# A gated message pass over 25,000 sorted edges: destination rows taken from the node pass by 0/1 products

## The reference

```python
h = jnp.maximum(_layernorm(x, axis=-1), 0.0)
concat = jnp.concatenate([h[src], h[dst], edge_attr], axis=-1)      # 96 + 96 + 64
gates = jax.nn.sigmoid(concat @ W_e + b_e)
messages = jax.nn.softplus(concat @ W_n + b_n)
gated = gates * messages
h_new = jax.ops.segment_sum(gated, dst, num_segments=n)
edge_count = jnp.clip(segment_sum(ones, dst), 1.0, None)
return x + h + h_new / edge_count
```

## Time and profile before

| what | value |
|---|---|
| three runs | 864.51, 865.22, 868.5 us; median 865.22 |
| the profiled execution | 866.81 us, of which the span is 865.0 us |
| busy share of the span | POOL 77%, ACT 67%, PE 66%, DVE 65% |
| mean granted TensorE clock | 0.741 of full speed |
| mean share of the 16 DMA engines | 36.8% on SP's queue q1, 10.7% on POOL's queue q0 |

### The profile page before, as it was taken

How to read it: one execution, slowest core, us unless ns; L and a number is a source line. 1 busy time by engine, 2 the same in 40 slices (tenths; PEclk the granted TensorE clock), 3 DMA queues, 4 the chain that set the end, 5 groups by cost and what they waited for, 6 DMA issues and landing times.

```text
span 865.0 us, 10598 instructions
## 1 busy us (share of the span) xinstructions
PE 569.3 (66%) x2360; PEld 447.4 (52%) x2360; DVE 560.8 (65%) x2397; ACT 583.2 (67%) x1475; POOL 668.3 (77%) x598
## 2 busy tenths in 40 slices
PE   0497775784666466988764665489966664569861
PEld 0376554564554355666553554367655543456650
DVE  5799977567756775677567756775577557754550
ACT  3699988757775777577757775777577756775440
POOL 4787778777777777777777877787778777877774
PEclk9999987768788777555788788755577788775575
DMA  6766655544554455445544554455445543532200
GB/s 215 218 208 192 190 183 147 189 126 125 152 187 125 125 155 184 125 124 149 189 128 123 152 186 127 125 147 189 129 124 147 187 129 125 159 99 80 72 31 23
DMA packets 67032, 125.23 MB, mean 145 GB/s; under 512 B 38167, under 2 KB 39049, under 8 KB 66968
## 3 DMA queue, kind: packets, MB, share of 16 engines
q1 hardware_dynamic: 47390, 96.48, 36.8%
q0 software_dynamic: 18816, 27.77, 10.7%
q10 hardware_dynamic: 762, 0.30, 0.1%
HBM read 77.50 MB, written 48.17 MB: 145 GB/s over the span
## 4 chain that ended last, share of the span: by engine, by line
POOL 74%; issue 20%; DMA 2%; POOLq 1%; DVE 1%; PE 0%; ACTq 0%; SPq 0%
POOL edge_x L324 53%; POOL out L341 22%; DMA out<-node_out 1%; DMA index_rows<-in_src 1%; POOLq L341 1%; DMA edge_x<-in_x,gather_idx 0%; POOLq L339 0%; DVE node_out L637 0%; DVE stats L663 0%; DVE final L575 0%; POOLq L321 0%; DVE softplus L705 0%; PE trans_ps L760 0%; ACTq L245 0%; DVE gather_idx L500 0%
## 5 line engine op out<-in xcount | busy, mean ns | idle before, releaser
L324 POOL DMA_INDIRECT edge_x<-in_x,gather_idx x392 | 469.1, 1197 | 128.2 <-issue 119.2
L398 ACT ACTIVATE node_out<-node_x,shift,rstd 128x96 f32<-128x96 f32 x686 | 279.0, 458 | 1.7 <-DVE shift L615 1.7
L793 PE MATMUL trans_ps<-ident,concat 128*128 128x128 f32 x392 | 92.7, 414 | 259.6 <-ACT concat L433 259.6
L341 POOL DMA_INDIRECT out<-final,scatter_idx x196 | 197.9, 1010 | 59.7 <-issue 58.5
L663 DVE BATCH_NORM_STATS2 stats<-edge_x 128x6 f32<-128x96 f32 x392 | 67.4, 245 | 258.6 <-DMA edge_x<-in_x,gather_idx 258.6
L809 PE MATMUL z_ps<-weights,concat_t 128*128 128x192 f32 x784 | 220.8, 414 | 0.0
L793 PEld LDWEIGHTS trans_ps<-ident,concat 128*128 128x128 f32 x392 | 73.9, 216 | 276.1 <-ACT concat L433 257.0
L809 PEld LDWEIGHTS z_ps<-weights,concat_t 128*128 128x128 f32 x784 | 151.1, 227 | 56.0 <-issue 56.0
L405 ACT ACTIVATE log_var<-var 128x24 f32<-128x24 f32 x51 | 11.4, 223 | 239.0 <-DVE var L685 239.0
L433 ACT ACTIVATE concat<-edge_x,shift,rstd 128x96 f32<-128x96 f32 x392 | 145.7, 456 | 2.7 <-DVE shift L615 0.7
L557 DVE BATCH_NORM_STATS2 stats<-node_x 128x6 f32<-128x96 f32 x784 | 142.6, 242 | 0.0
(11 more groups left out here) (68 smaller groups left out, 373.4 us busy)
## 6 DMA issues: line engine op xcount, KB each, us to landing
node_x<-in_x SPq DMA_DIRECT2D x49, 768.0 KB, 5.8
out<-node_out SPq DMA_DIRECT2D x49, 768.0 KB, 7.5
dst_across<-in_dst SPq DMA_DIRECT2D x48, 256.0 KB, 7.1
edge_x<-in_x,gather_idx POOLq DMA_INDIRECT x392
concat<-in_edge_attr SPq DMA_DIRECT2D x48, 128.0 KB, 6.3
out<-final,scatter_idx POOLq DMA_INDIRECT x196, 2.2
dst_across<-in_dst SPq DMA_DIRECT2D x1, 212.0 KB, 3.6
index_rows<-in_dst SPq DMA_DIRECT2D x2, 64.0 KB
```

Source lines behind the costliest of these rows:

```text
L324: nc.gpsimd.indirect_dma_start(out=edge_x[u][:, t, side, :], out_offset=None, in_=x, in_offset=bass.IndirectOffsetOnAxis(ap=gather_idx[:, ...
L341: nc.gpsimd.indirect_dma_start(out=out, in_=final[j % FINALS][:, t, :], in_offset=None, out_offset=bass.IndirectOffsetOnAxis(ap=scatter_id ...
L398: last = nc.scalar.activation(node_out[u][:, r, :], node_x[u][:, r, :], ACT.Relu, bias=shift[us][:, c:c + 1], scale=rstd[us][:, c:c + 1])
L793: last = nc.tensor.transpose(trans_ps[h][:, t, b, :], concat[uk][:, 2 * h + t, b * P:(b + 1) * P], ident[:, :])
```

## The change

- The gathers by `dst` go, with `base`. POOL issues four gathers a step, and `edge_x` holds only source rows.
- The scatters add to what the node pass has stored (`compute_op=ALU.add`) instead of overwriting, so the rows to write are the mean alone (one instruction, L717).
- h at the destinations comes from the node pass. A chunk is now laid out as 16 blocks of 128 consecutive nodes (block = row of the tile, node = partition). The low seven bits of each destination are stored once to `low_pad` and, for each half chunk, 400 of them from the first edge of the half on are copied to all partitions (`low_across`). DVE compares them with the partition's number (`one_hot`, 800 columns). PE multiplies each block of h (as stationary operand) with 64 columns of that 0/1 matrix (`picks`, L950), at an offset read from a table of places into registers, and ACT copies each half's 336 columns to `dst_t` (L502), in which h of the destination stands transposed for `z`.
- `z` is made of three products: source rows with a row of ones for the bias (97 rows, L1016), destination rows (96, L1017), attributes (128 rows, two tiles' worth with half of the weights zero, L1018).
- Node chunks are moved in pieces of one node row, 384 bytes, 2,048 for each chunk.
- `same_prev` compares only the last 32 edges of a tile with the first 32 of the next. `dst_across` has two buffers where it had four, and SP issues it for batch `i-7` where it was `i-3`. `LEAD` is 3, the node sum is a step further ahead, three node rows of 16 are DVE's.
- A start-up part finds where each block's edges begin (`places`), and the slow path computes its messages anew.

```diff
-LEAD = 2
+LEAD = 3
-BY_DVE = 2
+BY_DVE = 3
+WINDOW = 64
+REACH = 336
+SPAN = REACH + WINDOW
-            first = min(i * CHUNK, NODES - CHUNK)
-            return t[first:first + CHUNK, :].rearrange("(p r) d -> p r d", p=P)
+                parts = [(t[lo:lo + CHUNK, :].rearrange("(r p) d -> p r d", p=P), tile[:, :, :])]
...
+            def load_low(n):
+                first, second = (first_at(sp, first_row[0:1, 2 * n + h:2 * n + h + 1]) for h in range(2))
+                wait(sp, onehot_done, n)
+                for h, at in ((0, first), (1, second)):
+                    sp.dma_start(low_across[:, h, :],
+                                 low_flat[bass.ds(at, SPAN)].partition_broadcast(P)).then_inc(low_loaded, 16)
...
+                n = i - 2
+                if i >= NS - 1 and runs_step(n):
+                    load_low(n)
-                k, ok, uk = back(i, o, u, LEAD + 1)
+                k = i - 7
                 if runs_step(k):
-                    wait(sp, same_done, k - NS + 1)
+                    wait(sp, same_done, 2 * (k - 1))
...
-                    wait(pool, base_done, i - NS + 1)
+                    wait(pool, edge_norm_done, i - NS + 1)
                     for t in range(TB):
-                        for side in range(2):
-                            nc.gpsimd.indirect_dma_start(
-                                out=edge_x[u][:, t, side, :], out_offset=None, in_=x,
+                        nc.gpsimd.indirect_dma_start(
+                            out=edge_x[i % NS][:, t, :], out_offset=None, in_=x,
...
-                            bounds_check=NODES - 1, oob_is_err=False).then_inc(scattered[j % FINALS], 16)
+                            bounds_check=NODES - 1, oob_is_err=False, compute_op=ALU.add).then_inc(scattered[j % FINALS], 16)
...
+            def pick_columns(d, h, at):
+                wait(act, pick_done, 2 * d + h + 1)
+                nc.scalar.activation(dst_t[0:D, bass.ds(at, REACH)], pick_ps[0:D, 0:REACH], ACT.Copy).then_inc(pick_out, 1)
...
+            def one_hot(n):
+                wait(dve, low_loaded, 32 * (n + 1))
+                wait(dve, pick_done, 2 * (n - 1))
+                nc.vector.tensor_scalar(onehot[n % 2][:, :, :], low_across[:, :, :], lane[:, 0:1], None,
+                                        ALU.is_equal).then_inc(onehot_done, 1)
...
+                k, j, m = i - 1, i - 2, i - 3
+                c, n, d = i + LEAD, i - 1 + LEAD, i - 2 + LEAD
...
                 if now:
-                    last = node_stats(uc, 3, R)
-                if runs_step(k):
-                    nc.vector.tensor_tensor(base[uk][:, :, :], edge_x[uk][:, :, 1, :], concat[uk][:, :, D:2 * D],
-                                            ALU.add).then_inc(base_done, 1)
+                    last = node_stats(c, 3, R)
+                if runs_step(n):
+                    one_hot(n)
+                if runs_step(d):
+                    wait(dve, pick_done, 2 * d + 2)
+                    nc.vector.tensor_tensor(node_out[d % NS][:, :, :], node_out[d % NS][:, :, :], node_x[d % NS][:, :, :],
+                                            ALU.add).then_inc(node_sum_done, 1)
...
+            def picks(d, h, at):
+                wait(pe, pick_out, 2 * d + h)
+                for b in range(BLOCKS):
+                    a = at[h * BLOCKS + b]
+                    last = nc.tensor.matmul(pick_ps[0:D, bass.ds(a, WINDOW)], node_out[d % NS][:, h * BLOCKS + b, :],
+                                            onehot[d % 2][:, h, bass.ds(a, WINDOW)], start=True, stop=True)
+                last.then_inc(pick_done, 1)
...
-                            nc.tensor.matmul(z, ones[0:1, :], bias[0:1, :], start=True, stop=False)
-                            for b in range(2):
-                                last = nc.tensor.matmul(z, concat_t[:, h, t, b, :], weights[:, b, :], start=False, stop=(b == 1))
+                        nc.tensor.matmul(z, src_t[0:D + 1, t, :], w_src[0:D + 1, :], start=True, stop=False)
+                        nc.tensor.matmul(z, dst_t[0:D, e:e + P], w_dst[0:D, :], start=False, stop=False)
+                        last = nc.tensor.matmul(z, attr_t[:, t // 2, :], w_attr[t % 2][:, :], start=False, stop=True)
```

More of the change, by code:

```diff
@@ L218, in last_rows @@
             return i == STEPS - 1
-        def first_steps(step):
-            for i in range(-LEAD, 0):
-                step(i, i // NS, i % NS)
         def ends(i, passed):
@@ L298, in _ @@
+            for i in range(STEPS + 7):
+                step(i)
             for u in range(NS):
-                sp.wait_ge(node_stored[u], 16 * ((STEPS - 1 - u) // NS + 1))
+                sp.wait_ge(node_stored[u], chunk_dmas(STEPS - 1 - (STEPS - 1 - u) % NS))
         @block.gpsimd
@@ L762, in _ @@
                 nc.tensor.transpose(cols_ps[n][:, P:TILES], index_rows_f[0:k, n, 1, :], ident[0:k, 0:k]).then_inc(cols_done, 1)
-            pe.wait_ge(cols_read, 2)
-            pe.wait_ge(message_ones_done, 1)
-            pe.wait_ge(weights_loaded, 16 * 4)
+            pe.wait_ge(cols_read, 1)
+            nc.tensor.matmul(heads_ps, ones[0:1, :], dst_col[0:1, 1:1 + TILES], start=True, stop=True).then_inc(heads_done, 1)
+            place_regs = [pe.alloc_register(f"place{b}") for b in range(R)]
@@ new lines, in step @@
+                if runs_step(d):
+                    if d == 0:
+                        pe.wait_ge(place_loaded, 32)
+                        pe.wait_ge(ones_done, 2)
+                    pe.load(place_regs, place_row[0:1, d * R:(d + 1) * R])
+                    at = [pe.snap(r, min_val=0, max_val=REACH) for r in place_regs]
+                    wait(pe, node_norm_done, d + 1)
+                    wait(pe, dve_norm_done, d + 1)
+                    wait(pe, onehot_done, d + 1)
+                    picks(d, 0, at)
@@ L798, in step @@
+                    last.then_inc(attr_trans_done, 1)
+                if runs_step(d):
+                    picks(d, 1, at)
                 if runs_step(m) and not ends(i, 1):
@@ L812, in step, with later_sums @@
                     sums(i - 2)
-            steps(step, 2)
+            for i in range(-LEAD, STEPS + 2):
+                step(i)
             pe.wait_ge(flag_done, 1)
             bad = pe.value_load(flag[0:1, 0:1], min_val=0, max_val=1)
-            def tile_sums(t, n):
+            def later_sums(n):
                 pe.wait_ge(r_diag_done, n + 1)
```

790 lines of the change are left out of this document (500 added, 290 removed).

## The result

| | kernel before | changed kernel |
|---|---|---|
| median of runs | 865.8 us (864.51 to 868.5, 4 runs) | 949.6 us (948.0 to 955.4, 4 runs) |
| ratio | 1 | 1.098 (95% interval 1.092 to 1.103) |
| span of the profiled execution | 865.0 us | 949.3 us |
| granted clock, mean | 0.741 | 0.792 |

Ratios in this document leave out executions that took over 1.5% more than the fastest of the same kernel on the same chip, so they can differ a little from a ratio of medians.

The account below looks back on a forecast made before the run. SP's loop through DVE was to bound each step: 8.8 + 1.6 + 1.05 = 11.4 (L) plus 6.0 (M) = 17.4 us. Start 81, 42 rounds 731, three short 39, end 37: 888 us, 2.6% slower; range 800 to 1,000.

Parts of the forecast that it names:

- Loop through SP, T = L + M: SP and DVE: node sum to `dst_across` landing (L, 11.4 us) plus comparison to node sum (M, 6.0) makes 17.4 a step.
- L of before, 8.8 us: In the kernel before, `node_x` issue to `dst_across` landing, taken from the old trace as 8.8 us.
- Small pieces, +1.6 us at 22 ns a piece: Chunk loads and stores in 384-byte pieces: 256 on each DMA engine take 5.6 us against 4.05, adding 1.6 to L.
- The first rival: Small chunk pieces cost only their bytes, 15.8 ns each: L 9.9, T 15.8, total 811 us; chance 0.22.
- the price doubled for stores: Rival: chunk stores in 384-byte pieces cost twice 22 ns, adding 2.8 us a step, about 1,010 us in total; chance 0.07.
- `low_across`, +1.05 us: Two `low_across` loads in SP's queue, 0.41 MB at 388 GB/s, add 1.05 us to L.
- M = 6.0: DVE's work from the comparison to the node sum's end, 0/1 matrix included, takes 6.0 us (5.4 to 6.1).
- Register loads at nothing: SP's register loads fall while its queue is full of the store's pieces: no cost; without that cover up to 2 us.
- Adding scatters cost POOL no change: On POOL, a scatter that adds takes no longer than a plain one, about 1.0 us; upper bound 2.1.
- The start, 81: Start-up: first node sum at 42 us, three more by the loop through `low_across` at 13 us each, ending at 81.
- PE at the low clock: Rival: half of the steps take PE's low-clock 21.2 us, half 17.4, so T is 19.3 and the total 976; chance 0.17.
- Loop doesn't hold: Rival: `dst_across` lands in time, the loop through `low_across` sets 13.4 us a step, total 708 us; chance 0.10.

Follow-up runs that it names:

- three ways of opening it: Changed kernel with `dst_across` one step earlier, 797 us; with it ahead of `low_across`, 843; with both ahead of SP's wait for the node sum, 734 to 740.
- the first four experiments: Changed kernel: `dst_across` a step earlier, 796.7 us; `dst_across` ahead of `low_across`, 843.1; both ahead of SP's wait, 740.3; chunks in 6,144-byte pieces, 884.6.

## Why the prediction was half right

- **Loop through SP, T = L + M.** Right. The waits, the chain, SP's issue at the very end of each node sum, and three ways of opening it (797, 843 and 734 to 740 us) show it. POOL, ACT, DVE don't bind, as worked out; POOL's 12.3 us a step (12.8 by the scatters' measured 1.58) would have mattered only without the loop.
- **L of before, 8.8 us.** Right: 8.80 with both additions taken out, though it was put together from one step's issues and a median landing.
- **Small pieces, +1.6 us at 22 ns a piece.** Near, with some luck: 1.53 with `low_across` in the queue, 1.1 without. A chunk's pieces take 6.6 us of the engines and not 5.6 (22 ns is their median, 25.7 their mean), and in large pieces 5.3 and not 4.05, so both were too low and the difference is 1.3. This and `low_across` are why the share of q1 is 52.8% and not the 40 to 45 named as a sign. The first rival (pieces at the price of their bytes) is out. So is the price doubled for stores: it would have added 2.8 us, and the whole cost of loads and stores in small pieces is 1.5; the first half of a round's small pieces, the load in the queue's order, takes 25.2 ns each and the second, the store, 26.2. The Trainium skill's rule on transfers below 512 bytes (DMA: Bandwidth & Descriptors, section Specifications) is not contradicted in its direction, since large pieces are faster, but no doubling shows.
- **`low_across`, +1.05 us.** This is the step that failed: "2 x 128 x 1,600 bytes = 0.41 MB at 388 GB/s: +1.05. It is larger pieces, so the full rate fits." It measures 2.1 to 2.54 us in L, and 2.45 by the time of its pieces: 153 ns for one where 388 GB/s would be 66. The rate came from a stretch of whole chunks, and unlike the small pieces this term got no range. A better row of the old trace would not have helped: `dst_across`, the broadcast there, ran at the full rate, 85 ns for 2,048 bytes. What the old trace could not show is how a broadcast runs in the new place, behind a store in small pieces, where `dst_across` is slow too (140 ns). The run with one transfer of 3,200-byte pieces gave 0.9 us back, so part of the price lies in the number of pieces or of transfers; the rest of the cause stays open. Both additions are 3.65 us where 2.65 was forecast, and M gives 0.1 back: 0.9 us in each of 42 rounds, the +39.
- **M = 6.0.** Right, 5.89, by two misses that nearly cancel: by their starts the 0/1 matrix takes 0.54 us and not 0.9, and the two comparisons 1.04 and not 0.79.
- **Register loads at nothing.** Right, and for the reason given.
- **Adding scatters cost POOL no change.** Wrong in size, 1.58 us against 1.0, though inside the bound of 2.1. In the rounds POOL has the room and L loses 0.3 at most; the end pays. Behind the last node sum there are 24 scatters, and 16 of them run back to back, at 0.57 us more each: 9 us. In the runs with plain scatters the end is 44 us and not 49, so some 5 us of the +12 are theirs by that; the rest is open. I had let POOL's spare time in the rounds stand for the end, where it has none.
- **The start, 81.** 8 us short, over eight steps that no row showed.
- **PE at the low clock.** Did not come: a granted clock of 0.792 and 51 us of ACT and DVE waiting for picks in all. "Loop doesn't hold", 708 us, did not come either; opening the loop by hand gives 734 to 740.

## What to carry to other kernels

When a change puts an issue behind a wait on a queue, look for the loop (what releases the queue, what stands behind the release, who needs what stands there and how long after) and compare the order on both sides: here a transfer needed 5 us after its release made a loop where one needed 15 us after did not. Here the place of three issues was worth more than the whole change, 9.8% slower against 15% faster. A row for a transfer holds for the place in the queue in which it was measured: behind other traffic it is a low bound, so give the term a range. And cost the end of a kernel by itself, since an engine's spare time in the rounds isn't there.

## What the runs showed of the hardware

- Two reads of one DRAM row into 128 partitions, 1,600 bytes each, took 2.1 to 2.5 us in a full queue for 0.41 MB (160 to 195 GB/s); one read of 3,200 bytes 0.9 us less. Rows of a chunk in 384-byte pieces moved at about 300 GB/s next to them. Pieces of 2,048 bytes of such a read took 85 ns each behind a chunk in large pieces, the full rate of 388 GB/s, and 140 behind one in small pieces. Neither size nor kind of piece alone is a measure.
- An indirect scatter that adds moves row by row: the software queue has 22,019 packets of 384 bytes, about one for each row with edges, and 34,576 in all. Without the add, with the same gathers, there are none of that size and 12,624 in all:

```profile
q0 software_dynamic: 12624, 18.39, 6.7%
```

  and POOL pays 1.58 us in place of 1.00 for 128 rows of 384 bytes.
- An issue on SP's queue lasts longer behind many pieces: 0.43 us for a store in 128 pieces, 1.67 to 2.04 for one in 2,048, and right behind that store 3.16 for one broadcast (0.45 behind the store in 128 pieces) and 3.67 for two.
- The same kernel took 865 us in two measurements and 943 to 1,005 on four other chips, with pauses of PE that the 865 us traces don't have. The changed kernel took 951 on one of those four. A ratio to the kernel before holds for its chip alone: by it, the first four experiments are 10 to 25% gains over the kernel before, while against 865 us three of them gain 3 to 14% and one, 884.6, loses 2%.
